# Attention: the layout of the stored inverse sums, from token by token to column by column

## The reference, cut to what matters

```
xn, ln = layernorm(context), layernorm(layernorm(x))        # per sequence
q = ln @ Wq ; k, v = split(concat(xn, ln) @ Wkv)            # 16 heads of 64
w = softmax(q k^T / 8) ; out = (w v) @ Wo ; x = x + out     # 128 queries, 256 keys
```

## Time and profile before

| | us |
|---|---|
| median of three runs (lowest to highest) | 3171.97 (3169.43 to 3172.02) |
| profiled execution | 3171.49 |
| its span | 3169.8 |
| PE busy, span | 2871.4 |
| POOL busy, span | 2006.3 |
| DVE busy, span | 2375.1 |
| ACT busy, span | 1759.9 |
| `scale_heads`, L697, 128 times | 139.9 |

### The profile page before, as it was taken

One profiled execution on the slowest core, in us unless ns is written; L12 is line 12 of the kernel. 1 busy time (PEld: TensorE's weight loads), 2 busy tenths in 40 slices (PEclk: granted clock), 3 DMA queues, 4 the chain that ended last, 5 costly groups with the idle time before them and its releaser, 6 DMA issues. The chain is left out here.

```text
span 3169.8 us, 61556 instructions
## 1 busy us (share of the span) xinstructions
PE 2871.4 (91%) x21070; PEld 2473.1 (78%) x21070; DVE 2375.1 (75%) x5003; ACT 1759.9 (56%) x4520; POOL 2006.3 (63%) x1983
## 2 busy tenths in 40 slices
PE   6999999999999999999979999999999943179897
PEld 5888888888888888888868888888888831057675
DVE  5767777677776777777647877878778659889997
ACT  5666666666766666666643333332333326089997
POOL 4888888888888888888853333343333310069887
PEclk9999999999999999999989999999999965589999
DMA  8665655566566665666651111121211260001111
GB/s 216 114 114 108 115 109 115 112 111 117 109 111 117 111 117 105 111 112 113 111 130 58 48 59 60 48 75 44 70 53 51 68 113 1 8 27 47 48 34 41
DMA packets 704757, 272.16 MB, mean 86 GB/s; under 512 B 606168, under 2 KB 667328, under 8 KB 704448
## 3 DMA queue, kind: packets, MB, share of 16 engines
q1 hardware_dynamic: 704448, 268.23, 40.6%
HBM read 120.16 MB, written 13.73 MB: 42 GB/s over the span
## 5 line engine op out<-in xcount | busy, mean ns | idle before, releaser
L843 POOL COPY attention_probT<-attention_planesT 128x1024 uint16<-128x1024 uint16 x512 | 677.7, 1369 | 180.1 <-PE attention_turns L421 102.4
L528 ACT ACTIVATE attention_prob<-attention_turns,attention_neg_max 128x256 f32<-128x256 f32 x1024 | 467.6, 481 | 224.4 <-DVE attention_neg_max L681 214.7
L1434 POOL TENSOR_TENSOR experts_hidden_lo<-experts_weighed,experts_hidden_hi 128x512 fp32r<-128x512 f32 x192 | 254.9, 1328 | 531.4 <-ACT experts_hidden_hi L1187 531.4
L834 POOL COPY attention_planes<-attention_prob 128x1024 uint16<-128x1024 uint16 x512 | 526.6, 1059 | 20.9 <-ACT attention_prob L528 20.9
L681 DVE TENSOR_REDUCE attention_neg_max<-attention_turns 128x2 f32<-128x512 f32 x512 | 317.7, 682 | 176.9 <-PE attention_turns L406 176.8
L382 PE MATMUL attention_turns<-kv_hi,wkv 128*128 128x512 f32 x1024 | 375.0, 407 | 0.0
L1187 ACT ACTIVATE experts_hidden_hi<-experts_weighed 128x512 fp32r<-128x512 f32 x192 | 121.4, 632 | 404.1 <-DVE experts_weighed L1324 404.1
L350 PE MATMUL attention_turns<-wkv,kv_hi 128*128 128x512 f32 x1024 | 315.5, 389 | 1.9 <-ACT attention_prob L528 1.9
L421 PE MATMUL attention_turns<-attention_probT,attention_v 128*64 128x128 f32 x4096 | 255.6, 278 | 3.1 <-issue 3.1
L697 DVE TENSOR_TENSOR attention_turns<-attention_turns,attention_attT_lo 128x512 f32<-128x512 f32 x128 | 139.9, 1093 | 152.0 <-DMA attention_attT_lo<-inverse_rows 150.3
L517 ACT COPY attention_v<-attention_turns 128x512 f32<-128x512 f32 x256 | 150.4, 589 | 184.5 <-PE attention_turns L350 184.5
(11 more groups left out here) (297 smaller groups left out, 8596.4 us busy)
## 6 DMA issues: line engine op xcount, KB each, us to landing
attention_attT_lo<-inverse_rows SPq DMA_DIRECT2D x256, 128.0 KB, 3.0
experts_spread<-shares SPq DMA_DIRECT2D x256, 128.0 KB, 3.0
attention_ctx<-in_ctx SPq DMA_DIRECT2D x32, 256.0 KB, 3.2
attention_planesT<-attention_planes SPq DMA_TRANSPOSE x512, 3.2
experts_far_ctxT<-in_ctxT SPq DMA_DIRECT2D x32, 256.0 KB, 3.4
weights_ctx<-in_ctx SPq DMA_DIRECT2D x16, 512.0 KB, 3.8
out<-conv_x_out SPq DMA_DIRECT2D x15, 512.0 KB, 2.8
x_all<-in_x SPq DMA_DIRECT2D x7, 1024.0 KB, 9.1
```

The lines of the kernel that those rows point to most:

```text
L528: made = act.activation(prob[n % 2][:, h, :], bank_of("s", 2 * n + e)[:, m * 256:(m + 1) * 256], ACT.Exp, bias=neg_max[:, n % 2, 2 * e + m ...
L834: pool.tensor_copy(planes[n % 2][:, g, :, :], words.rearrange("p (c b) -> p b c", b=2)).then_inc(planes_made, 1)
L843: pool.tensor_copy(words.rearrange("p (c b) -> p b c", b=2), planesT[:, g, :, :]).then_inc(joined, 1)
L1434: pool.tensor_tensor(hid_lo[n % 3][:, :], weighed[n % 2], hid_hi[n % 3][:, :].bitcast(F32), ALU.subtract).then_inc(hid_split, 1)
```

## The change

The inverses are stored in device memory as (o, c, t) instead of (o, t, c). Store, load and reader follow. The memory in `inv_cols` then has the 128 inverses of a column c contiguous.

```
-    inv_rows = nc.dram_tensor("inverse_rows", (2, 2, TOK, 4), F32, kind="Internal").ap()
+    inv_rows = nc.dram_tensor("inverse_rows", (2, 2, 4, TOK), F32, kind="Internal").ap()

             def store_inverses(u):
-                sp.dma_start(inv_rows[u % 2].rearrange("o t c -> t o c"),
-                             inv[:, u % 2, :, :, :].rearrange("p o e m -> p o (e m)")).then_inc(inv_stored, 16)
+                sp.dma_start(inv_rows[u % 2].rearrange("o c t -> t o c"),
+                             inv[:, u % 2, :, :, :].rearrange("p o e m -> p o (e m)"),
+                             allow_slow_non_contiguous=True).then_inc(inv_stored, 16)

             def load_inverses(w):
-                                 inv_rows[w % 2, o:o + 1].rearrange("o t c -> o (t c)").broadcast_to([HEAD, 4 * TOK])
+                                 inv_rows[w % 2, o:o + 1].rearrange("o c t -> o (c t)").broadcast_to([HEAD, 4 * TOK])

             def scale_heads(w):
-                dve.tensor_tensor(bank, bank, inv_cols.rearrange("p (t c) -> p c t", c=4), ALU.mult).then_inc(scaled, 1)
+                dve.tensor_tensor(bank, bank, inv_cols.rearrange("p (c t) -> p c t", c=4), ALU.mult).then_inc(scaled, 1)
```

## The result

The changed kernel takes 3598.71 us (median of four runs, 3593.34 to 3604.28), the kernel before beside it 3171.99. The ratio is 1.133, 95% interval 1.1315 to 1.1347: 427 us slower, where a gain of 8.5 us was forecast, and far outside the range of 3159 to 3177.

What follows compares the result with a forecast made beforehand. TensorE was taken to bound the attention, with 18 us idle. The reader's terms (6.5, 0.8, 0.4, 0.8) sum to 8.5 us, store and load 0: 3171.49 - 8.5 = 3163.0, about 3163.5 in comparison; range 3159 to 3177.

Steps and rivals of the forecast that it cites:

- What bounds the kernel: Attention: TensorE busy 1481.90 of 1500 us, so a faster VectorE can give back no more than 18 us there.
- the gaps at a change of pair: TensorE before a round's first scores: 16 gaps, 16.9 us together, shortened by 6.5 us through a faster `scale_heads`.
- Part 1, the reader: `scale_heads` on VectorE: contiguous reading saves 0.41 us each time, 8.5 us of it on the path.
- the gap at 92.62: One more TensorE gap before scores, 0.68 us long, to be shortened by 0.4 us.
- the wait before the transposes of the inputs: TensorE's 3 gaps ended by VectorE's normalised latents, 1.1 us together, to shrink by 0.8 us.
- the 0.8 us at the end of the stage: Rounds no longer overlapped: two TensorE waits for `attT_lo`, each chain with one `scale_heads`, two times 0.41 us saved.
- Rival B: `scale_heads`: the 1093 ns come from writing PSUM, so no gain, 3171.5 to 3172; chance 0.12.
- rival C: VectorE's queue: normalisations meeting more of a POOL copy give half the gain back, 3167; chance 0.20.
- Part 2, the store: Inverse store in 1024 runs of 4 bytes: 0.60 us per DMA engine fits the 0.75 us of room, cost 0.
- The upper end of 22 ns: Store's high price per packet, from 256-byte transpose packets: 1.41 us per DMA engine, 0.66 us of delay.
- Rival A: End of each pair: small writes hold up the queue, 3175 to 3179, or 3198 to 3223 at 44 ns; chance 0.13.
- Nobody waits for the store itself: SP's queue: the store's load comes two rounds later; only transposes and the inverse load stand behind it.

Runs made afterwards that it cites:

- reader alone: The kernel before with only the reader changed to (c, t), store and load as they were: ratio 0.9979, a gain of 6.7 us.
- x4far: The kernel before plus a second store to a scratch tensor, 1024 runs of 4 bytes, 64 bytes apart: ratio 1.0011.
- x4_own: The kernel before plus a second store, 1024 runs of 4 bytes, 8 bytes apart, one token's 8 values side by side: ratio 1.0387.
- x4near: The kernel before plus a second store to a scratch tensor, 1024 runs of 4 bytes, adjacent: ratio 1.1855.

## Why the prediction was wrong

- **What bounds the kernel, and the gaps at a change of pair:** right. The reader alone shortened them from 16.9 to 10.5 us; the list of what would show it said "about 10".
- **Part 1, the reader, 0.41 us each and 8.5 us in all:** right in the mechanism and near in the size. It was 0.39 us each and 6.7 us in all (3.8 to 9.5) by the reader alone. In its profile the gaps before the scores gave 6.4 of the 6.5 us and the gap at 92.62 is gone, but the wait before the transposes of the inputs fell only from 1.1 to 1.0 us where 0.8 were summed, and the 0.8 us at the end of the stage aren't seen (the waits for `attT_lo` behind 1600 us were 20.1 us, before 16.4). The choice of 0.41 called 1093 ns "nearly twice" the other row; it is 1.6 times. The run agrees with the rule of the Trainium skill ("SBUF — State Buffer", section "Door 1: The DMA port swizzle") on 16-byte lines: with the step gone, the same result in PSUM takes 699 ns. Rival B (the write to PSUM is what costs) has fallen. Of rival C the profile shows nothing: the normalisations of the stage take 946 ns in the mean against 942. The measured gain alone would not exclude its 4 to 5 us.
- **Part 2, the store:** this step failed: "Value taken for the whole store: 0", from 9.4 ns for each packet and thus 0.60 us of the DMA engines in a room of 0.75 us. The count of 1024 packets was right, and its sentence that a tiny packet should cost the same at 4 or 16 bytes holds where the writes lie apart (x4far). What does not hold is the other half of that sentence, that this is "the same write to the same place". Adjacent in device memory the writes take 10.2 us by themselves, 7.7 more than spread out. The upper end of 22 ns came from packets of 256 bytes that go to SBUF, all to different places. It was no bound on writes that share a place, and the range rested on it. With 9.4 to 22 ns I bounded the cost per packet, when the question was how many of them go to the same place: 4 tokens for each 64 bytes before, 16 after. The prediction had that fact in rival A ("16 neighbours in device memory come from different tokens now") and gave it no price.
- **Rival A** had the sign and the first half of the mechanism, with a chance of 0.13, but its place and price were too small. It let the store delay the inverse load at the end of a pair, and thought the other three rounds safe, since TensorE has no gap there. It did not look at the loop of transposes and joins, which has some 3 us of slack in every round (12.46 against twice 4.8). The transposes behind the store landed 6.9 us later than the 3.2 before. Such a delay uses up the slack, and the rest lengthens the round, not only at the end of a pair. At 44 ns the rival said 3198 to 3223; the store's 7.7 us are worth 7.7 / 64 = 120 ns per packet of an engine. It would be tempting to add these 7.7 us to the 0.61 x 12.46 = 7.6 us of DMA share in a round: 15.3, close to the measured 15.72. But the sum doesn't carry over. It gives 7.6 + 3.2 = 10.8 us for x4_own, below the 12.46 of TensorE and thus no loss, and the round took 13.40; for x4near about 15.3, and it took 17.01. That the DMA engines are full is not shown.
- **Nobody waits for the store itself:** nearly true, and beside the point. The profile lays 9 waits of the inverse load, 30.8 us in 1500, at the store's landing; what the others waited for is the landing of their own transfers behind it.

## What to carry to other kernels

A store that puts one element of every partition side by side in device memory is not a matter of so many small packets: here writes into the same few hundred bytes waited for each other and held up the transfers behind them, on their own queue and on the other one. To see what a late transfer costs, look for the loop it stands in (buffer, transfer, the engine that frees the buffer) and for that loop's slack, not for the engine that is busiest. Before a layout is turned in the DMA, turn the order in which the engine walks its operands; for VectorE a step of 512 bytes in PSUM was free where the same walk in SBUF with a step of 16 bytes cost 56%. And when a price has to be bounded by the nearest rows, ask in what the new case differs from all of them (here the destination), and leave the range open there.

## What the hardware showed that I had not expected

- 128 writes of 4 bytes into 512 adjacent bytes take 8.6 us, the same 64 bytes apart 1.4 us, and eight such columns side by side 10.2 us.
- The DMA share of a window is no measure of what the engines move: 1.37 at 48 GB/s in the stalled piece, 1.03 at 190 GB/s in transposes before the change, and 0.01 from 2.05 to 3.05 us after the issue of the small writes, which need 9.4 us or more to land even when they are alone.
- VectorE reads PSUM and writes it back in place with a step of 512 bytes at the same rate (700 ns for 512 elements) as contiguous (699); in SBUF a step of 8 bytes is free (699 ns) and one of 16 bytes isn't (1093).
